# Two graph layers with residual and layer norm, 8192 nodes: the first of four in-place sums of tile quarters goes from VectorE's queue to GpSimd's

## The reference, cut to what matters

```python
N, D = 8192, 64                            # x: N x D; adj: N x N, float32; u: N x D
x_drop = x * (u >= 0.1) / 0.9
x = layernorm(x + adj @ x_drop)            # layer 1, gives h
x = layernorm(x + adj @ (x @ weight) + bias)   # layer 2
return x
```

## Time and profile before

| what | value |
|---|---|
| median of three runs | 892.34 us (892.27 to 892.49) |
| time of the profiled execution | 892.4 us |
| its span, first to last instruction | 890.6 us |
| granted TensorE clock, mean | 0.996 |
| TensorE matmul busy | 859.6 us, 97% |
| VectorE busy | 553.2 us, 62% |
| GpSimd busy | 25.3 us, 3% |
| DMA, mean | 402 GB/s, 357.63 MB |

### The profile page before, as it was taken

The page is one execution under the profiler, slowest core; times in us unless marked ns, Lnnn a source line. Parts: engine busy times, 40 slices in busy tenths (PEclk is TensorE's granted clock), DMA queues, the critical chain, the costliest instruction groups (busy, mean ns, idle before and its releaser), DMA issues.

```text
span 890.6 us, 15637 instructions
## 1 busy us (share of the span) xinstructions
PE 859.6 (97%) x6742; PEld 498.5 (56%) x6742; DVE 553.2 (62%) x1132; ACT 25.5 (3%) x63; POOL 25.3 (3%) x24
## 2 busy tenths in 40 slices
PE   2899899999999999999999999999999999999996
PEld 2565564445576676675756464564645645556432
DVE  6366123145135676787677777776877868787755
ACT  2100000000000000000000000000000000000011
POOL 3000000000000000000000000000000000000133
PEclk9999999999999999999999999999999999999998
DMA  9999999999999999999999999999989999999972
GB/s 373 413 415 420 422 421 419 421 421 420 420 410 424 419 421 421 418 420 368 422 421 420 407 421 379 423 390 394 422 363 421 421 418 421 420 420 421 421 299 71
DMA packets 53108, 357.63 MB, mean 402 GB/s; under 512 B 6192, under 2 KB 8240, under 8 KB 10288
## 3 DMA queue, kind: packets, MB, share of 16 engines
q1 hardware_dynamic: 53040, 356.64, 96.9%
HBM read 354.52 MB, written 2.10 MB: 400 GB/s over the span
## 4 chain that ended last, share of the span: by engine, by line
PE 91%; DMA 5%; SPq 1%; issue 1%; DVE 1%; POOLq 0%; POOL 0%; ACT 0%; DVEq 0%
PE psum L1031 22%; PE psum L984 22%; PE psum L999 8%; PE psum L967 8%; PE psum L993 8%; PE psum L1017 8%; DMA tiles<-adj_chunks 5%; PE psum L953 4%; PE psum L974 4%; PE psum L1037 4%; PE psum L930 1%; SPq L499 1%; PE psum L995 1%; PE psum L969 1%; PE psum L1001 1%
## 5 line engine op out<-in xcount | busy, mean ns | idle before, releaser
L984 PE MATMUL psum<-tiles,stat 128*64 128x256 f32 x1952 | 218.0, 379 | 0.0
L1031 PE MATMUL psum<-tiles,stat 128*64 128x512 f32 x944 | 210.0, 593 | 0.0
L656 DVE TENSOR_TENSOR layer<-psum,layer 128x512 f32<-128x512 f32 (+1 forms) x147 | 101.4, 690 | 170.3 <-PE psum L1017 65.2
L984 PEld LDWEIGHTS psum<-tiles,stat 128*64 128x64 f32 x1952 | 158.2, 137 | 59.4 <-issue 8.6
L1031 PEld LDWEIGHTS psum<-tiles,stat 128*64 128x64 f32 x944 | 70.8, 137 | 117.1 <-issue 113.5
L692 DVE TENSOR_TENSOR tiles<-tiles 128x512 f32<-128x512 f32 x86 | 59.4, 691 | 52.1 <-PE psum L976 50.6
L1001 PE MATMUL psum<-tiles,stat 128*64 128x256 f32 x344 | 88.5, 380 | 0.0
L969 PE MATMUL psum<-tiles,stat 128*64 128x256 f32 x344 | 88.3, 379 | 0.0
L967 PE MATMUL psum<-tiles,stat 128*64 128x256 f32 x344 | 88.3, 379 | 0.0
L1017 PE MATMUL psum<-tiles,stat 128*64 128x512 f32 x320 | 70.4, 593 | 3.1 <-issue 3.1
L967 PEld LDWEIGHTS psum<-tiles,stat 128*64 128x64 f32 x344 | 47.1, 137 | 34.9 <-issue 16.5
(11 more groups left out here) (99 smaller groups left out, 866.5 us busy)
## 6 DMA issues: line engine op xcount, KB each, us to landing
tiles<-adj_t SPq DMA_DIRECT2D x306, 1024.0 KB, 13.0
tiles<-adj SPq DMA_DIRECT2D x12, 1024.0 KB, 19.3
tiles<-adj_chunks SPq DMA_DIRECT2D x12, 1024.0 KB, 21.4
tiles<-xu SPq DMA_DIRECT2D x4, 1024.0 KB, 8.1
tiles<-adj_parts SPq DMA_DIRECT2D x16, 256.0 KB, 17.9
out<-layer SPq DMA_DIRECT2D x8, 256.0 KB, 2.2
w<-weight SPq DMA_DIRECT2D x4, 16.0 KB, 9.0
bias_b<-bias SPq DMA_DIRECT2D x1, 32.0 KB, 9.4
```

The source lines that it names most:

```text
L656: return dve.tensor_tensor(out=to, in0=addend, in1=to, op=ALU.add)
L984: last = pe.matmul(sum_f[i % 2][to, left], stat[:, j * C + c, 0:D], tile[:, c, columns], start=begun.get("f") != i and c == 0, stop=ends a ...
L1031: last = pe.matmul(bank[to, :], stat[:, j * C + c, D:2 * D], tile[:, c], start=c == 0, stop=c == C - 1)
```

## The change

The wait for the tile and the first sum leave VectorE's queue and go, as a plain loop over the 86 "fused" tiles in their order, into GpSimd's queue between its setting up and its work of the last rows. The gating by `AHEAD` and the row's end is gone: GpSimd waits for nothing but the tile's arrival. Sums 2 to 4 stay on VectorE, in the same places, and wait for `first_sums_ready` as before. TensorE's, ScalarE's and SyncE's queues are the same.

```diff
-AHEAD = 3
...
-            first_sums_from.append(min(raw_done, max(raw_done - AHEAD, freed_for[job[1:3], "raw"], chain_at)))
-            second_sums_from.append(raw_done)
+    second_sums_from = [done_after["raw", *job[1:]] for job in fused_jobs]
...
             pool.memset(mean_of_partitions, 1.0 / P).then_inc(identity, 1)
+            for job in fused_jobs:
+                slot, load = place[job, job[1:3]]
+                tile, right = tiles[:, slot], slice(B // 2, B)
+                pool.wait_ge(s_arrived[slot], 16 * load)
+                pool.tensor_tensor(out=tile[:, 0:2, right], in0=tile[:, 0:2, right], in1=tile[:, 2:4, right],
+                                   op=ALU.add).then_inc(first_sums_ready, 1)
             pool.wait_ge(weights_centred, 2)
...
-            def first_sums(n):
-
-                slot, load = place[fused_jobs[n], fused_jobs[n][1:3]]
-                tile, right = tiles[:, slot], slice(B // 2, B)
-                dve.wait_ge(s_arrived[slot], 16 * load)
-                dve.tensor_tensor(out=tile[:, 0:2, right], in0=tile[:, 0:2, right], in1=tile[:, 2:4, right],
-                                  op=ALU.add).then_inc(first_sums_ready, 1)
...
-                    while n_second_sums < len(fused_jobs):
-                        if n_second_sums < n_first_sums and second_sums_from[n_second_sums] <= n_tile_jobs:
-                            second_sums(n_second_sums)
-                            n_second_sums += 1
-                        elif n_first_sums < len(fused_jobs) and first_sums_from[n_first_sums] <= n_tile_jobs:
-                            first_sums(n_first_sums)
-                            n_first_sums += 1
-                        else:
-                            break
+                    while n_second_sums < len(fused_jobs) and second_sums_from[n_second_sums] <= n_tile_jobs:
+                        second_sums(n_second_sums)
+                        n_second_sums += 1
```

More of the change, by code:

```diff
@@ L658, in _ @@
             n_tile_jobs = 0
-            n_first_sums = n_second_sums = 0
+            n_second_sums = 0
             n_combined = 0
```

## The result

The changed kernel takes 902.1 us in the median of four runs (901.67 to 903.66), the kernel before 892.41 us: a ratio of 1.0112, with a 95% interval of 1.0099 to 1.0125. It is slower by 9.7 us where 4.4 were forecast, and above the range's end of 900.5. The profiled execution took 903.66 us, with a span of 901.9. It is the slowest of the four, so its losses are 1.6 us larger than the median's.

What follows compares the result with a forecast made beforehand. TensorE was taken as the bound, busy in all 625 us. From 892.4 us, minus 0 for VectorE's relief, plus 4.4 for the engines blocking each other, gave 896.8, or 896.7 as median of the runs; range 892.0 to 900.5.

Steps and rivals of the forecast that it cites:

- the relief of VectorE: 86 first sums, 57.9 us, leave VectorE, which is off the path: gain nothing, 1.6 us at most.
- The first sum is never late: On GpSimd, sum 1 is ready earlier than before and costs TensorE nothing.
- the direction that no row of before showed: GpSimd's sum first and VectorE's blocked: taken as symmetrical, from nothing to a whole GpSimd sum per encounter.
- the one term, 4.4 us: GpSimd's first sums delay VectorE's sums 2 to 4 at 27 places with one short job between, costing TensorE 4.4 us.
- The first is this: Between VectorE's overlapping sums 3 and 4 no GpSimd sum gets in; a GpSimd sum that comes then waits.
- The bound for both boundaries: If GpSimd gets in at both boundaries between sums 2 to 4, 2.2 us more, 6.6 us in all.
- the middle of the two rows: Length of GpSimd's first sum: 1.15 us, between two similar GpSimd lines at 1043 and 1274 ns.
- the price of a full block: A GpSimd sum getting in ahead of a VectorE sum delays it by a whole GpSimd sum, 1.15 us.
- The second premise: First sums on GpSimd start at landings unrelated to TensorE's jobs, at a mean rate of 0.138 per us.
- rival 2 of the prediction: Landings come in bunches together with the tight sums: loss 13 us (905), up to 27 us (919); chance 0.08.
- A third step: A delay d of sums 2 to 4 costs TensorE d - 0.2 us at 22 places and d at 5.
- wide: 58 of 86 places with two jobs between raw and fused: slack 1.48 us, more than a GpSimd sum, nothing lost.

Runs made afterwards that it cites:

- beside memsets: The kernel before, with GpSimd clearing a spare array three times per landed fused tile (writes only): 892.44 us against 892.35.
- with more slack: The changed kernel with each raw job one more job ahead of its fused job: 893.2 us, against 892.0 for the kernel before in that order.
- the two delayed versions: The changed kernel with one or three clearings of a spare array on GpSimd between each landing and first sum: 903.85 and 900.98 us.
- the one on the five places: The changed kernel with the raw job moved one job ahead at five tight places without slack alone: 901.18 us against 892.3.

## Why the prediction was wrong

**What held.** The kernel is bound by TensorE in this stretch, and the relief of VectorE is worth nothing (892.27 us without the first sums). The first sum is never late. The loss is the two engines blocking each other, in both directions: the direction that no row of before showed is in the timeline at 470.54. That was the rule of the Trainium skill, page "SBUF — State Buffer", section "Who interferes with whom": two SBUF inputs on VectorE against a GpSimd instruction that reads SBUF, not one that only writes. The runs agree on each part: 1.07 us blocked, 0.69 us kept by L649, 892.44 us beside memsets. And the loss is paid at the 27 places with one short job between "raw" and "fused": 9.7 us fall to 1.2 with more slack, and of the 10.6 us that TensorE loses at "fused" jobs in the profiled execution 10.2 lie at these.

**What failed** is the size of the one term, 4.4 us, by two of its premises. The first is this: "L695 and L697 are only 0.61 us apart with 0.69 us each, so they overlap, and I take it that nothing gets in between". GpSimd gets in there too; L682 (L697 of before) is stretched five times. These are the eleven places in the profiled execution at which TensorE lost more than 0.15 us, read from the timeline against the same places before, by the sum that was stretched:

| stretched | places | TensorE lost | in the forecast |
|---|---|---|---|
| sum 2 | 6 | 4.0 us | 1.8 us |
| sum 3 | 3 | 3.8 us | 2.6 us |
| sum 4 | 2 | 2.1 us | 0 |

Unrounded that is 10.0 us of the 11.2 of this execution. The bound for both boundaries was in the prediction (6.6 us), but I took the middle, and ended the range at 8.1 us over before. The length of GpSimd's sum was mis-sized as well: 1.275 us in the median, that of L530 to the hundredth, not the middle of the two rows (with 1.27 us its own working gives 5.1 us, where it says 5.2). Of that 1.1 us block VectorE at most (1.80 - 0.69), so the price of a full block was nearly right at 1.15. With a block of 1.1 us and both boundaries, the prediction's own working gives 22 x (0.9²/2 + 1.3 x 0.9) + 5 x (1.1²/2 + 1.3 x 1.1) = 44.8 us², times 0.138 = 6.2 us. Over the change and the two delayed versions the mean loss is (9.7 + 11.4 + 8.6) / 3 = 9.9.

The second premise accounts for most of the 3.7 us between: "Sum 1 starts when a tile lands, at a time unrelated to TensorE's jobs", and so at the mean rate of 0.138 per us. The timelines of these three kernels, place by place against before, say otherwise (mean loss of the three profiled executions, whose whole mean is 10.5 us):

| places | TensorE lost over 0.15 us | mean loss | by the working |
|---|---|---|---|
| 5 without slack | 13 times of 15 | 5.2 us | 1.4 us |
| 9 with 0.2 us, not the row's last "fused" | 16 times of 27 | 4.1 us | 4.8 us, with the 13 |
| 13 with 0.2 us, the row's last "fused" | 0 times of 39 | 0 | |
| the 59 others | | 0.5 us | 0 |

At the last "fused" of each of the 13 rows no first sum starts within 5 us of sum 2, in any of the three. At the other 14 places neighbouring fused tiles are landing. At the five they come for the most part 2.5 us apart, about as long as the 1.1 + 1.3 = 2.4 us in which a start holds up the sums. At the mean rate a place without slack would be met with 0.138 x 2.4 = 0.33; TensorE lost time there 13 times of 15 (once only because VectorE came late), and a shift of 0.5 or 1.5 us only brought the next landing in. So rival 2 of the prediction was in part right, at five places. The trace of before could have told: by the landings recorded in it, a fused tile lands from 1.3 us ahead of sum 2 to 1.3 us after it at ten of the 27 places, and all ten are among the eleven of the table above.

A third step was wrong in kind: "A delay d of sums 2 to 4 costs TensorE d - 0.2 us at 22 places and d at 5" takes each place by itself. A delay at a place with slack can reach the next through VectorE's queue. VectorE, kernel after:

```profile
741.16 1.75 DVE L677 TENSOR_TENSOR tiles<-tiles 128x512 f32<-128x512 f32 x1 [2.73 <-PE psum L955]
742.95 0.69 DVE L680 TENSOR_TENSOR tiles<-tiles 128x512 f32<-128x512 f32 x1
743.56 0.69 DVE L682 TENSOR_TENSOR tiles<-tiles 128x512 f32<-128x512 f32 x1
744.16 0.68 DVE L649 TENSOR_TENSOR layer<-psum,layer 64x512 f32<-64x512 f32 x1
744.87 0.69 DVE L812 TENSOR_TENSOR layer<-psum,layer 64x512 f32<-64x512 f32 x1
745.48 0.68 DVE L677 TENSOR_TENSOR tiles<-tiles 128x512 f32<-128x512 f32 x1
746.19 1.69 DVE L680 TENSOR_TENSOR tiles<-tiles 128x512 f32<-128x512 f32 x1
```

And GpSimd and TensorE there:

```profile
741.10 1.27 POOL L509 TENSOR_TENSOR tiles<-tiles 128x512 f32<-128x512 f32 x1 [6.86 <-DMA tiles<-adj_t]
743.58 1.79 POOL L509 TENSOR_TENSOR tiles<-tiles 128x512 f32<-128x512 f32 x1 [1.22 <-DMA tiles<-adj_t]
746.07 1.27 POOL L509 TENSOR_TENSOR tiles<-tiles 128x512 f32<-128x512 f32 x1 [0.70 <-DMA tiles<-adj_t]
```

```profile
746.30 0.40 PE L972 MATMUL psum<-tiles,stat_homes 128*64 128x256 f32 x1 [0.55 <-DVE tiles L677]
...
748.54 0.43 PE L978 MATMUL psum<-tiles,stat_homes 128*64 128x256 f32 x1 [1.15 <-DVE tiles L682]
```

The first L677 stands for 1.1 us, which its own tile can bear; behind it the two joins push the second L677 back, and there another GpSimd sum comes in. This one place costs some 2 us, in the first table under sum 3. The tiles land 2.48 us apart here. Of the 15 chances at places without slack four cost more than one block, 1.5 to 2.1 us; that is some 0.9 us of the mean of 5.2.

**What stays open.** The three timelines say where the excess lies, and no run removed it there alone: the one on the five places brought the median down by 0.9 us only, though its traced execution lost 3.4 us less at these five. The 0.5 us at other places aren't traced in full; two of the 58 places that the prediction took for wide have some 0.6 us of slack (0.69 and 0.71 us from the end of sum 4 to its use, less 0.06), not 1.48, and lost up to 0.6 us. Another 0.7 us of the 10.5 lie outside the "fused" jobs. The 1.2 us that are left with more slack aren't traced to a row either.

## What to carry to other kernels

Before work is moved to an idle engine, ask for what it will meet there: a two-input GpSimd sum (1.27 us) held up two-input VectorE sums in SBUF by up to 1.1 us, and got in at each boundary between them, even where they overlap. What this costs is set by the slack behind VectorE's result, not by the blocked time: 24 us of stretching cost 11.2 us in the profiled execution, with 0.2 us of slack or none at 27 places, and 32 us cost 1.2 us with more. Where starts follow landings, don't take a mean rate: lay the landings in the trace beside the tight places. If the move is wanted all the same, tie the start of GpSimd's instruction to the end of VectorE's group, with a spare period between (892.97 us), not to a landing (902.1) and not to the event that releases VectorE too (905.25).

## What was not expected of the hardware

GpSimd got in between two VectorE instructions whose records overlap (starts 0.61 us apart, 0.69 us each); a back-to-back queue doesn't keep it out. An addition of one array to itself took 1.04 us on GpSimd in the median, against 1.27 for the two-array sum, at the same size. VectorE's short instructions outside the tile sums were held up as well: one that subtracts arrays of 128 x 128 (L665 of the changed kernel) took 0.29 us at the least and 1.39 at the most.
